# First of the four additions over the states by an accumulating DMA issued from the Pool engine; two state tiles, and the rest of each sum one chunk later

## The chip, the cores and the metric

One Trainium2 chip, one core. The metric is device microseconds of one execution of the whole program, the median of several runs. The core has five engines, each with a program of its own that runs in order: TensorE (PE), VectorE (DVE), ScalarE (ACT), GpSimd (POOL) and SyncE (SP, which here only issues DMAs). They meet through semaphores: `wait_ge(s, v)` holds an engine, and all that stands behind it there, until `s` has reached `v`.

## The reference, cut to what matters

Three blocks with residuals: attention to a context, a selective scan (Mamba), and a feed-forward block with quantised weights. The change is in the scan and at the three layer norms.

```python
x = x + attention(ctx, ctx, _layernorm(x), mask, ...)       # 64 sequences of 32, 257 keys, 16 heads of 32
x = x + mamba(_layernorm(x), ...)
x = x + ffn(_layernorm(x), ...)                             # 512 -> 2048 -> 512, quantised

# mamba: d_inner 1024, 16 states n for each channel d
dt  = softplus(bcd[..., -1:] * dt_w + dt_b)
dA  = exp(dt[..., None] * A)
dBx = (dt * x_)[..., None] * Bm[:, :, None, :]
def step(h, inp):
    dA_t, dBx_t, C_t = inp
    h = dA_t * h + dBx_t
    y_t = einsum('bdn,bn->bd', h, C_t)                      # the sum over the 16 states
    return (h, y_t)
y = (y + x_ * D) * silu(z);  out = y @ out_proj_w
```

## The kernel before, in words

**Tiles.** The 2048 rows are cut into 16 tiles of 128 rows, that is 4 sequences each. One tile passes attention, then the scan, then its output product. `schedule` is one list of steps that every engine walks in the same order, each doing its own part of a step (`part.x` does nothing on an engine that has no method of that name). `interval(ta, tm, to, more)` works at three tiles at once: attention of tile `ta`, the first part of the scan of `tm = ta - 1`, the end of the scan and the output of `to = ta - 2`. It has four quarters b = 0 to 3, one for each sequence. The intervals for `ta` = 0, 1, 2 are written out, 3 to 14 are a hardware loop, 15 is written out again, and two more intervals without attention empty the pipe. Afterwards the feed-forward block runs over all rows.

**The scan.** The 1024 channels of a tile are 8 chunks c of 128 channels, one for each partition. A chunk takes four steps on DVE, which this text calls:
- B(c), L1442: `hb` = u times the rows B, 128x2048 (16 states of 128 positions);
- S(c), L1446: the scan over `hb` in place with the decays `dA` of the chunk, 128x2048;
- C(c), L1451: `hb` times the rows C, 128x2048;
- sum(c), L1457 and L1461: the sum over the 16 states by four halvings, of 1024, 512, 256 and 128 elements; the last writes `u`.

There is one `hb`, so the 32 steps of a tile run strictly one after the other (step k is step k % 4 of chunk k // 4). The decays are 16 exponentials of 128x124 a chunk on ACT (`decays`, L1141), in two tiles `dA`: those of chunk c wait for S(c - 2).

**Where the steps stand.** `place(name)` is called at named points of a quarter, and two tables say which scan steps stand there: `BEGIN` holds steps 0 to 13 of tile `tm` (from quarter 2 on), `FINISH` holds steps 14 to 31 of tile `to` (from quarter 0 on). The other DVE work between them is the attention's scores (`score_pass`, L1353, four passes with the key mask `maskn`) and reciprocals, `x1_write` (L1380, the attention's output plus the residual), the layer norm statistics (L1273, L1278), the convolution (L1407, 24 small instructions), `mamba_steps` (L1415, the 8 products that open the time steps dt) and `mamba_dt` (L1421, L1426), which closes them and makes `u`, and `mamba_gated` (L1468, L1471).

**Layer norm.** DVE takes the statistics of 128 rows, POOL makes scale and offset from them (`rstd`: L1187, L1189, L1192, three instructions on 128x1), ACT normalises the rows into one third of `ln_out` (L1019), and PE transposes them. The norm ahead of the scan (index 1) stands in quarter 0: `x1_write`, statistics, `rstd`, ACT, transpose (L867), the product with `win_sb` (`in_product`, L874), ACT's copies and first taps (L1088), DVE's convolution. POOL also scales the key mask once a quarter (L1201), adds the residual's bias (L1215), and copies x1 into x2 (`mamba_keep`, L1241), for which the next `x1_write` waits.

**The row dt.** In quarter 1 `mamba_bcd` copies the small product (L1101) and SP sends it to DRAM and its last row back to all partitions (`BC`, 64 KB), which `mamba_steps` in quarter 2 reads.

```python
for b in range(BT):
    ...
    if b == 0 and front: part.mamba_norm(tm)
    place("a")
    if here: part.softmax(g)
    place("m")
    if b == 0 and front: part.mamba_rows(tm)
```

## Time and profile before

| | us |
|---|---|
| median of 3 runs (lowest, highest) | 2366.3 (2363.32, 2367.36) |
| the profiled execution, its own time | 2362.47 |
| its span, first to last instruction | 2360.7 |
| DVE busy | 2020.6 (86% of the span) |
| PE busy | 1942.2 (82%) |
| ACT busy | 1676.1 (71%) |
| POOL busy | 344.0 (15%) |
| granted TensorE clock, mean | 0.914 of full speed |
| DMA queue q1, share of 16 engines' time | 17.8% |

All durations come from the one profiled execution; what lies around its span is 1.8 us. In forty equal slices of it DVE is busy 90% or more from the fifth slice to the thirty-seventh nearly throughout, and PE, with 80 to 99%, is hardly less so until the attention ends. With three engines so full, the share of busy time doesn't tell which one sets the pace: the chain of waits and the engines' timelines over one interval do. The timelines below are those of one pass of the loop, between 1170 and 1300 us, and of the last two intervals, after 2018 us. All passes of the loop look alike.

### The profile page before, as it was taken

How to read it: one execution, taken by the hardware profiler on the slowest of the kernel's cores; microseconds unless marked ns; L12 is line 12 of the kernel's file. 1: busy time of each engine (PE TensorE's matmuls, PEld its weight loads, DVE VectorE, ACT ScalarE, POOL GpSimd, SP SyncE). 2: the span in 40 equal slices, each digit the busy share in tenths (PEclk: the TensorE clock that was granted, in tenths of full speed). 3: DMA queues.
4: the chain of work that ended last, by engine and by line, in shares of the span. 5: the costliest groups of instructions: out<-in, count | busy, mean ns of one | idle time of the engine just before them, and what ended most of it. 6: DMA issues, size and time to landing. Idle time of an engine off the chain costs nothing.

```text
span 2360.7 us, 36464 instructions
## 1 busy us (share of the span) xinstructions
PE 1942.2 (82%) x11244; PEld 1371.5 (58%) x11244; DVE 2020.6 (86%) x2429; ACT 1676.1 (71%) x4598; POOL 344.0 (15%) x296
## 2 busy tenths in 40 slices
PE   6998898989798888989898989798888987430678
PEld 5676566666575666666666666575656665320233
DVE  1534989999999999999999999999999999899577
ACT  2457787877878787778787877878887878653391
POOL 1000121121211111111111111212111111000003
PEclk9999998989999999989999989999999998765789
DMA  7521010111111101112121211111111211210113
GB/s 224 221 74 65 25 66 26 64 37 60 41 55 39 46 37 36 64 37 64 34 66 25 64 37 60 41 60 34 48 36 35 64 32 42 77 42 22 56 37 120
DMA packets 81206, 136.48 MB, mean 58 GB/s; under 512 B 17408, under 2 KB 40592, under 8 KB 75920
## 3 DMA queue, kind: packets, MB, share of 16 engines
q1 hardware_dynamic: 81040, 134.89, 17.8%
q14 instruction: 138, 1.13, 0.2%
q8 instruction: 28, 0.46, 0.1%
HBM read 117.69 MB, written 17.18 MB: 57 GB/s over the span
## 4 chain that ended last, share of the span: by engine, by line
DVE 31%; ACT 23%; PE 15%; issue 12%; DMA 3%; POOL 2%; DVEq 1%; ACTq 0%; SPq 0%; POOLq 0%
ACT dA L1141 10%; DVE hb L1446 10%; PE bank L874 6%; DVE hb L1457 5%; DVE hb L1451 5%; DVE hb L1442 3%; PE bank L944 2%; PE bank L784 2%; DVE xs L1407 2%; DMA BC<-bcd_dram 2%; ACT Pr L1012 2%; ACT Pr L1045 2%; PE bank L954 1%; ACT KT L990 1%; DVE dt L1415 1%
## 5 line engine op out<-in xcount | busy, mean ns | idle before, releaser
L1141 ACT ACTIVATE dA<-dt,A_sb 128x124 f32<-128x124 f32 x2048 | 610.6, 390 | 91.7 <-DVE dt L1421 58.6
L1446 DVE TENSOR_TENSOR_SCAN hb<-dA,hb 128x2048 f32<-128x2048 f32 x128 | 566.1, 4423 | 21.4 <-ACT dA L1141 17.1
L775 PE MATMUL bank<-ctxT,wk_sb 128*128 128x256 f32 x2048 | 489.1, 398 | 65.3 <-ACT ctxT L982 62.8
L775 PEld LDWEIGHTS bank<-ctxT,wk_sb 128*128 128x128 f32 x2048 | 403.2, 200 | 139.2 <-ACT ctxT L982 60.4
L784 PE MATMUL bank<-wv_sb,ctxT 128*128 128x512 f32 x1024 | 462.1, 594 | 0.9 <-ACT ctxT L982 0.9
L1457 DVE TENSOR_TENSOR hb<-hb 128x1024 f32<-128x1024 f32 (+2 forms) x384 | 301.8, 786 | 12.2
L1451 DVE TENSOR_TENSOR hb<-hb,BC 128x2048 f32<-128x2048 f32 x128 | 296.9, 2319 | 6.3 <-issue 3.4
L874 PE MATMUL bank<-xn2T,win_sb 128*128 128x128 f32 x2048 | 269.5, 299 | 36.0 <-ACT xn2T L1070 31.7
L784 PEld LDWEIGHTS bank<-wv_sb,ctxT 128*128 128x128 f32 x1024 | 186.4, 191 | 193.8 <-issue 192.5
L1442 DVE TENSOR_TENSOR hb<-u,BC 128x2048 f32<-128x2048 f32 x128 | 293.2, 2291 | 3.4
L874 PEld LDWEIGHTS bank<-xn2T,win_sb 128*128 128x128 f32 x2048 | 266.2, 215 | 41.6 <-ACT xn2T L1070 36.2
L1187 POOL TENSOR_SCALAR stats<-stats 128x1 f32<-128x1 f32 x48 | 68.1, 1419 | 1028.4 <-DVE stats L1278 1028.4
L908 PE MATMUL bank<-wout_sb,zs 128*128 128x512 f32 x256 | 118.4, 617 | 95.0 <-DVE zs L1471 95.0
L1012 ACT ACTIVATE Pr<-Pr,soft 128x257 f32<-128x257 f32 x256 | 127.3, 508 | 48.6 <-DVE soft L1353 48.6
L990 ACT ACTIVATE KT<-bank,bqkv 128x256 f32<-128x256 f32 x256 | 106.4, 466 | 56.5 <-PE bank L775 54.9
L997 ACT COPY V<-bank 128x512 f32<-128x512 f32 x128 | 74.8, 584 | 101.0 <-PE bank L821 76.7
L1353 DVE CUSTOM_DVE_ANT_0 Pr<-bank,maskn 128x257 f32<-128x257 f32 x256 | 94.2, 421 | 61.0 <-PE bank L803 39.3
L821 PEld LDWEIGHTS bank<-PT,V 128*128 128x128 f32 x1024 | 125.9, 194 | 31.3 <-issue 31.3
L1201 POOL TENSOR_SCALAR maskn<-maskb 128x257 f32<-128x257 f32 x64 | 87.4, 1366 | 378.0 <-DVE soft L1353 365.2
L1407 DVE SCALAR_TENSOR_TENSOR xs<-xpad,convw,xs 128x128 f32<-128x128 f32 x384 | 106.3, 346 | 40.8 <-ACT xs L1088 39.5
L908 PEld LDWEIGHTS bank<-wout_sb,zs 128*128 128x128 f32 x256 | 49.5, 199 | 152.8 <-DVE zs L1471 95.6
L821 PE MATMUL bank<-PT,V 128*128 128x128 f32 x1024 | 126.4, 277 | 0.8 <-ACT PT L1062 0.8
(131 smaller groups left out, 2357.6 us busy)
## 6 DMA issues: line engine op xcount, KB each, us to landing
ctx_sb<-in_ctx_dram SPq DMA_DIRECT2D x64, 512.0 KB, 3.7
BC<-bcd_dram SPq DMA_DIRECT2D x32, 1024.0 KB, 4.9
maskb<-in_mask_Bx1x1xS_fk_dram SPq DMA_DIRECT2D x64, 128.5 KB, 3.3
wstage<-in_L_ffn_w_dram SPq DMA_DIRECT2D x4, 2048.0 KB, 10.6
x_sb<-in_x_dram SPq DMA_DIRECT2D x16, 256.0 KB, 3.4
win_sb<-in_L_attn_in_proj_w_dram SPq DMA_DIRECT2D x1, 4096.0 KB, 25.2
bo_sb<-bias_dram SPq DMA_DIRECT2D x64, 64.0 KB, 2.1
x_dram<-x SPq DMA_DIRECT2D x16, 256.0 KB, 2.1
```

The source lines that it names most:

```text
L775: last = pe.matmul(bank[6 + j][:, (m % 2) * KF:(m % 2 + 1) * KF], wk_sb[:, c, m * P:(m + 1) * P], ctxT[:, c, :], start=(c == 0), stop=(c = ...
L784: last = pe.matmul(bank[h][:], ctxT[:, c, h * P:(h + 1) * P], wv_sb[:, c, :], start=(c == 0), stop=(c == DC - 1))
L821: last = pe.matmul(bank[4][:, m * P:(m + 1) * P], V[:, h, m * P:(m + 1) * P], PT[:, h, m, :], start=(h == 0), stop=(h == 1))
L874: last = pe.matmul(bank[6 + q % 2][:, e * P:(e + 1) * P], win_sb[:, c, n:n + P], xn2T[:, c, :], start=(c == 0), stop=(c == DC - 1))
L908: last = pe.matmul(bank[5][:], zs[:, c, :], wout_sb[:, c, :], start=(c == 0), stop=(c == IC - 1))
L1012: act.activation(Pr[:, m, :], Pr[:, m, :], ACT.Exp, scale=-1.0, bias=soft[:, 0, m:m + 1], accum_out=soft[:, 1, m:m + 1]).then_inc(exp_done, 1)
L1141: last = act.activation(dA[:, c % 2, n * BT:(n + 1) * BT, 1:], dt[:, c, :].rearrange("p (b s) -> p b s", s=S)[:, :, 1:], ACT.Exp, scale=A_ ...
L1407: dve.scalar_tensor_tensor(acc, src, tap, acc, ALU.mult, ALU.add).then_inc(conv_done, 1)
L1442: ins = dve.tensor_tensor(hb[:], u[:, c, :].unsqueeze(1).broadcast_to([P, NS, P]), BC[:, 0:NS, :], ALU.mult)
L1446: ins = dve.tensor_tensor_scan(flat, dA[:, c % 2].rearrange("p n s -> p (n s)"), flat, 0.0, ALU.mult, ALU.add)
L1451: ins = dve.tensor_tensor(hb[:], hb[:], BC[:, NS:2 * NS, :], ALU.mult)
L1457: dve.tensor_tensor(hb[:, 0:n, :], hb[:, 0:n, :], hb[:, n:2 * n, :], ALU.add).then_inc(sum_step, 1)
```

## The change

- A second state tile: `hb` is `[P, 2, NS, P]`, and chunk c works in tile c % 2.
- After C(c), for c = 0 to 6, POOL issues a DMA that adds the upper eight states of the tile to the lower eight (source and target 128x1024 in fp32, that is 512 KB read, and 512 KB read and written again). DVE's sum(c) starts with the halving of 512 and waits for that DMA's semaphore `hb_added`. For chunk 7 (`whole`) all four additions stay on DVE.
- A new order of the 32 steps, `CHAIN`: B(c), S(c), sum(c - 1), C(c). The tables `BEGIN` and `FINISH` are rewritten for it, and the waits that counted steps go by `DONE`.
- To make room, `ln_out` has one third of its size and the three layer norms take turns in it, with waits for the transposes that read it; the unused space `apart` goes; `last_vT` and `bias_rows` move into x1 and x2.
- The load of the first block of the feed-forward input moves from ahead of the last interval into it.

```diff
--- before.py
+++ after.py
-        ln_out = sb("ln_out", [P, 3, D])
+        ln_out = sb("ln_out", [P, D])
...
-        sb("apart", [P, 800])
 
         dA = sb("dA", [P, 2, NS * BT, S])
-        hb = sb("hb", [P, NS, P])
+        hb = sb("hb", [P, 2, NS, P])
-        last_vT = ln_out[:, 2, 0:DC * B].rearrange("p (m b) -> p m b", b=B)
-        bias_rows = ln_out[0:B, 1, :]
-        hb_words = hb[:].rearrange("p n q -> p (n q)").bitcast(BF16)
+        last_vT = x1[:, 0:DC * B].rearrange("p (m b) -> p m b", b=B)
+        bias_rows = x2[0:B, :]
+        hb_words = hb[:, 0].rearrange("p n q -> p (n q)").bitcast(BF16)
...
+        CHAIN = [(0, 0), (0, 1), (0, 2)]
+        for c in range(1, IC):
+            CHAIN += [(c, 0), (c, 1), (c - 1, 3), (c, 2)]
+        CHAIN.append((IC - 1, 3))
+        DONE = {step: k + 1 for k, step in enumerate(CHAIN)}
...
-        FINISH = {(0, "a"): range(14, 15), (0, "b"): range(15, 17), (0, "c"): range(17, 21), (0, "e"): range(21, 22),
+        FINISH = {(0, "a"): range(14, 15), (0, "b"): range(15, 16), (0, "c"): range(16, 20), (0, "e"): range(20, 22),
...
+                    if b == 2 and back and not front:
+                        part.ffn_prefetch()
...
-                        sp.wait_ge(scan_step, 4 * IC * t - 3 + 2 * i)
+                        sp.wait_ge(scan_step, 4 * IC * (t - 1) + DONE[IC - 1, 2 * i])
...
+                    sp.wait_ge(scan_step, 4 * IC * (NT - 1) + DONE[IC - 1, 1])
                     sp.dma_start(xblk[:], xn3_dram[:, :, 0:TB]).then_inc(xb_loaded, 16)
...
-                def layernorm_rows(self, i, t, rows, used):
+                def layernorm_rows(self, i, t, rows):
                     act.wait_ge(ln_rstd[i], 3 * (t + 1))
-
-                    wait(act, used, t)
-                    act.activation(ln_out[:, i, :], rows, ACT.Identity, scale=stats[:, i, 9:10],
+                    act.activation(ln_out[:], rows, ACT.Identity, scale=stats[:, i, 9:10],
                                    bias=stats[:, i, 10:11]).then_inc(ln_done[i], 1)
 
                 def ln_q_rows(self, t):
-                    self.layernorm_rows(0, t, x_sb[:], xnT_psum)
+                    wait(act, xn2T_psum, t - 1)
+                    self.layernorm_rows(0, t, x_sb[:])
 
                 def mamba_rows(self, t):
                     if isinstance(t, int) and t == 0:
                         act.wait_ge(bias_stored, 16)
-                    self.layernorm_rows(1, t, x1[:], xn2T_psum)
+                    wait(act, xnT_psum, tiles(t + 2))
+                    wait(act, xn3T_psum, t - 1)
+                    self.layernorm_rows(1, t, x1[:])
 
                 def out_rows(self, t):
-                    self.layernorm_rows(2, t, x2[:], xn3T_psum)
+                    wait(act, xnT_psum, tiles(t + 4))
+                    wait(act, xn2T_psum, tiles(t + 2))
+                    wait(act, xn3T_psum, t)
+                    self.layernorm_rows(2, t, x2[:])
...
-                                act.wait_ge(scan_step, 4 * IC * t + 4 * (c - 2) + 2)
+                                act.wait_ge(scan_step, 4 * IC * t + DONE[c - 2, 1])
                             elif not first:
-                                act.wait_ge(scan_step, 4 * IC * t - 6 + 4 * c)
+                                act.wait_ge(scan_step, 4 * IC * (t - 1) + DONE[IC - 2 + c, 1])
...
+                def scans(self, t, steps):
+                    for k in steps:
+                        c, op = CHAIN[k]
+                        if op == 2 and not whole(c):
+                            pool.wait_ge(scan_step, 4 * IC * t + k + 1)
+                            apart(pool)
+                            pool.dma_start(hb[:, c % 2, 0:NS // 2, :], hb[:, c % 2, NS // 2:NS, :], accum_op=ALU.add
+                                           ).then_inc(hb_added, 16)
+
...
-                    flat = hb[:].rearrange("p n q -> p (n q)")
                     for k in steps:
-                        c = k // 4
-                        if k == 0:
-                            dve.wait_ge(u_ready, 2 * (t + 1))
-                            dve.wait_ge(bc_loaded[0], 16 * (t + 1))
-                            if isinstance(t, int) and t == 0:
-                                dve.wait_ge(wq_stored[3], 16)
-                        else:
-                            dve.wait_ge(scan_step, 4 * IC * t + k)
-                        if k % 4 == 0:
-                            ins = dve.tensor_tensor(hb[:], u[:, c, :].unsqueeze(1).broadcast_to([P, NS, P]),
+                        c, op = CHAIN[k]
+                        tile = hb[:, c % 2]
+                        flat = tile.rearrange("p n q -> p (n q)")
+                        if op == 0:
+                            if c == 0:
+                                dve.wait_ge(u_ready, 2 * (t + 1))
+                                dve.wait_ge(bc_loaded[0], 16 * (t + 1))
+                                if isinstance(t, int) and t == 0:
+                                    dve.wait_ge(wq_stored[3], 16)
+                            if c >= 2:
+                                dve.wait_ge(scan_step, 4 * IC * t + DONE[c - 2, 3])
+                            elif not (isinstance(t, int) and t == 0):
+                                dve.wait_ge(scan_step, 4 * IC * (t - 1) + DONE[IC - 2 + c, 3])
+                            ins = dve.tensor_tensor(tile, u[:, c, :].unsqueeze(1).broadcast_to([P, NS, P]),
                                                     BC[:, 0:NS, :], ALU.mult)
-                        elif k % 4 == 1:
+                        elif op == 1:
+                            dve.wait_ge(scan_step, 4 * IC * t + DONE[c, 0])
                             dve.wait_ge(dA_ready, IC * t + c + 1)
                             ins = dve.tensor_tensor_scan(flat, dA[:, c % 2].rearrange("p n s -> p (n s)"), flat, 0.0,
                                                          ALU.mult, ALU.add)
-                        elif k % 4 == 2:
-                            if k == 2:
+                        elif op == 2:
+                            dve.wait_ge(scan_step, 4 * IC * t + DONE[c, 1])
+                            if c == 0:
                                 dve.wait_ge(bc_loaded[1], 16 * (t + 1))
-                            ins = dve.tensor_tensor(hb[:], hb[:], BC[:, NS:2 * NS, :], ALU.mult)
+                            ins = dve.tensor_tensor(tile, tile, BC[:, NS:2 * NS, :], ALU.mult)
                         else:
-                            n = NS // 2
-                            for level in range(3):
-                                if level:
-                                    dve.wait_ge(sum_step, 3 * (IC * t + c) + level)
-                                dve.tensor_tensor(hb[:, 0:n, :], hb[:, 0:n, :], hb[:, n:2 * n, :], ALU.add
+                            dve.wait_ge(scan_step, 4 * IC * t + DONE[c, 2])
+                            if not whole(c):
+                                dve.wait_ge(hb_added, 16 * ((IC - 1) * t + c + 1))
+                            n = NS // 2 if whole(c) else NS // 4
+                            done = (2 * IC + 1) * t + 2 * c
+                            while n > 1:
+                                dve.tensor_tensor(tile[:, 0:n, :], tile[:, 0:n, :], tile[:, n:2 * n, :], ALU.add
                                                   ).then_inc(sum_step, 1)
+                                done += 1
+                                dve.wait_ge(sum_step, done)
                                 n //= 2
-                            dve.wait_ge(sum_step, 3 * (IC * t + c + 1))
-                            ins = dve.tensor_tensor(u[:, c, :], hb[:, 0, :], hb[:, 1, :], ALU.add)
+                            ins = dve.tensor_tensor(u[:, c, :], tile[:, 0, :], tile[:, 1, :], ALU.add)
                         ins.then_inc(scan_step, 1)
```

Three places in the order. First DVE in quarter 0, from the statistics of x1 on (tile `to` = 2 tiles back: C(3) comes first). Before:

```order
L1278 BN_AGGR stats<-stats 128x2
L1451 TENSOR_TENSOR hb<-hb,BC 128x2048
L1366 RECIPROCAL soft<-soft 128x4
L1457 TENSOR_TENSOR hb<-hb 128x1024
L1457 TENSOR_TENSOR hb<-hb 128x512
L1457 TENSOR_TENSOR hb<-hb 128x256
L1461 TENSOR_TENSOR u<-hb 128x128
L1442 TENSOR_TENSOR hb<-u,BC 128x2048
L1446 SCALAR_TENSOR_TENSOR hb<-dA,hb 128x2048
```

And in the changed kernel, where L1483 is C, L1472 is B, L1477 is S, and L1491 and L1496 are the sum:

```order
L1306 BN_AGGR stats<-stats 128x2
L1483 TENSOR_TENSOR hb<-hb,BC 128x2048
L1394 RECIPROCAL soft<-soft 128x4
L1472 TENSOR_TENSOR hb<-u,BC 128x2048
L1477 SCALAR_TENSOR_TENSOR hb<-dA,hb 128x2048
L1491 TENSOR_TENSOR hb<-hb 128x512
L1491 TENSOR_TENSOR hb<-hb 128x256
L1496 TENSOR_TENSOR u<-hb 128x128
L1483 TENSOR_TENSOR hb<-hb,BC 128x2048
L1472 TENSOR_TENSOR hb<-u,BC 128x2048
L1435 SCALAR_TENSOR_TENSOR xs<-xpad,convw,xs 128x128 x24
L1477 SCALAR_TENSOR_TENSOR hb<-dA,hb 128x2048
```

The four short additions of sum(3) behind C(3) have given way to B(4) and S(4), and sum(4), which stood ahead of the convolution, now stands behind it, ahead of the next scores. Second DVE in quarter 2, from the opening of dt to `mamba_gated`. Before:

```order
L1415 TENSOR_SCALAR dt<-BC,chan 128x128 x8
L1446 SCALAR_TENSOR_TENSOR hb<-dA,hb 128x2048
L1451 TENSOR_TENSOR hb<-hb,BC 128x2048
L1457 TENSOR_TENSOR hb<-hb 128x1024
L1457 TENSOR_TENSOR hb<-hb 128x512
L1457 TENSOR_TENSOR hb<-hb 128x256
L1461 TENSOR_TENSOR u<-hb 128x128
L1468 TENSOR_TENSOR u<-u,xD 128x1024
```

Now (L1443 is the opening of dt, L1503 the first of `mamba_gated`):

```order
L1443 TENSOR_SCALAR dt<-BC,chan 128x128 x8
L1477 SCALAR_TENSOR_TENSOR hb<-dA,hb 128x2048
L1491 TENSOR_TENSOR hb<-hb 128x512
L1491 TENSOR_TENSOR hb<-hb 128x256
L1496 TENSOR_TENSOR u<-hb 128x128
L1483 TENSOR_TENSOR hb<-hb,BC 128x2048
L1491 TENSOR_TENSOR hb<-hb 128x1024
L1491 TENSOR_TENSOR hb<-hb 128x512
L1491 TENSOR_TENSOR hb<-hb 128x256
L1496 TENSOR_TENSOR u<-hb 128x128
L1503 TENSOR_TENSOR u<-u,xD 128x1024
```

The sum of chunk 6 has come in behind S(7), and chunk 7 keeps all four of its additions. Third POOL in quarter 0 of the changed kernel (L1204 to L1209 are `rstd`, L1218 the mask, L1250 the zeros of the padding):

```order
L1232 TENSOR_TENSOR xbo<-x_sb,bo_sb 128x512
L1204 TENSOR_SCALAR stats<-stats 128x1
L1206 TENSOR_TENSOR stats<-stats,consts 128x1
L1209 TENSOR_SCALAR stats<-stats 128x1
L1243 DMA hb<-hb 128x1024
L1218 TENSOR_SCALAR maskn<-maskb 128x257
L1250 MEMSET xpad 128x32x3
L1243 DMA hb<-hb 128x1024
```

Before, the same stretch has the same rows without the two DMAs: the one for chunk 3 stands behind `rstd`, and the mask behind it.

## Rows read from the trace of the kernel before

**Rows 1.** The page: the chain that ended last, by engine and by line.

```profile
DVE 31%; ACT 23%; PE 15%; issue 12%; DMA 3%; POOL 2%; DVEq 1%; ACTq 0%; SPq 0%; POOLq 0%
ACT dA L1141 10%; DVE hb L1446 10%; PE bank L874 6%; DVE hb L1457 5%; DVE hb L1451 5%; DVE hb L1442 3%; PE bank L944 2%; PE bank L784 2%; DVE xs L1407 2%; DMA BC<-bcd_dram 2%; ACT Pr L1012 2%; ACT Pr L1045 2%; PE bank L954 1%; ACT KT L990 1%; DVE dt L1415 1%
```

**Rows 2.** Groups by line and form, DVE: busy us, mean ns, idle before.

```profile
L1457 DVE TENSOR_TENSOR hb<-hb 128x1024 f32<-128x1024 f32 x128 | 157.8, 1233 | 3.4
L1457 DVE TENSOR_TENSOR hb<-hb 128x512 f32<-128x512 f32 x128 | 88.6, 692 | 4.4
L1457 DVE TENSOR_TENSOR hb<-hb 128x256 f32<-128x256 f32 x128 | 55.4, 432 | 4.4
L1461 DVE TENSOR_TENSOR u<-hb 128x128 f32<-128x128 f32 x128 | 38.6, 301 | 4.4
```

**Rows 3.** Timeline of DVE, quarter 0: start us, duration us.

```profile
1266.20 0.66 DVE L1380 TENSOR_TENSOR x<-bank,xbo 128x512 f32<-128x512 f32 x1
...
1270.55 2.29 DVE L1451 TENSOR_TENSOR hb<-hb,BC 128x2048 f32<-128x2048 f32 x1
...
1272.87 2.41 DVE L1457 TENSOR_TENSOR hb<-hb 128x1024 f32<-128x1024 f32 x3
...
1275.72 2.29 DVE L1442 TENSOR_TENSOR hb<-u,BC 128x2048 f32<-128x2048 f32 x1
1278.13 4.42 DVE L1446 TENSOR_TENSOR_SCAN hb<-dA,hb 128x2048 f32<-128x2048 f32 x1
...
1291.08 6.74 DVE L1407 SCALAR_TENSOR_TENSOR xs<-xpad,convw,xs 128x128 f32<-128x128 f32 x24 [1.09 <-ACT xs L1088]
```

**Rows 4.** Timeline of POOL, quarters 3 and 0, and after the last scan.

```profile
1240.83 1.87 POOL L1241 COPY x<-x 128x512 f32<-128x512 f32 x1 [4.39 <-ACT ln_out L1019]
...
1270.87 2.05 POOL L1187 TENSOR_SCALAR stats<-stats 128x1 f32<-128x1 f32 x1 [0.81 <-DVE stats L1278]
1273.00 1.52 POOL L1189 TENSOR_TENSOR stats<-stats,consts 128x1 f32<-128x1 f32 x1
1274.73 0.27 POOL L1192 TENSOR_SCALAR stats<-stats 128x1 f32<-128x1 f32 x1 [0.21 <-POOL stats L1189]
...
2206.86 0.27 POOL L1192 TENSOR_SCALAR stats<-stats 128x1 f32<-128x1 f32 x1 [0.21 <-POOL stats L1189]
```

**Rows 5.** One line of POOL, `mamba_keep`: shortest, median and longest in ns.

```profile
L1241 POOL COPY x<-x x16: 611/1868/1871, 225.1 to 2109.5; 128x512 f32<-128x512 f32 x16
```

**Rows 6.** Timeline of ACT: the normalised rows of the scan's layer norm.

```profile
1275.12 0.81 ACT L1019 ACTIVATE ln_out<-x,stats 128x512 f32<-128x512 f32 x1 [4.38 <-POOL stats L1192]
```

**Rows 7.** Timeline of DVE, quarters 1 and 2.

```profile
1171.25 4.42 DVE L1446 TENSOR_TENSOR_SCAN hb<-dA,hb 128x2048 f32<-128x2048 f32 x1
1175.58 0.40 DVE L1353 CUSTOM_DVE_ANT_0 Pr<-bank,maskn 128x257 f32<-128x257 f32 x1
...
1201.21 2.14 DVE L1415 TENSOR_SCALAR dt<-BC,chan 128x128 f32<-128x128 f32 x8 [1.67 <-DMA BC<-bcd_dram]
```

**Rows 8.** Timeline of PE, quarter 1: the transposes of the attention weights.

```profile
1181.76 1.80 PE L812 MATMUL bank<-idf,Pr 128*128 128x128 f32 x8
```

**Rows 9.** Timeline of ACT, quarters 2 and 3: decays of chunks 0 and 2.

```profile
1216.03 4.74 ACT L1141 ACTIVATE dA<-dt,A_sb 128x124 f32<-128x124 f32 x16 [3.84 <-DVE dt L1421]
...
1247.29 2.43 ACT L1141 ACTIVATE dA<-dt,A_sb 128x124 f32<-128x124 f32 x8
```

**Rows 10.** Timeline of DVE, quarter 3: scans of chunks 1 and 2.

```profile
1237.87 4.42 DVE L1446 TENSOR_TENSOR_SCAN hb<-dA,hb 128x2048 f32<-128x2048 f32 x1
...
1249.98 4.42 DVE L1446 TENSOR_TENSOR_SCAN hb<-dA,hb 128x2048 f32<-128x2048 f32 x1
```

**Rows 11.** Timeline of DVE, the intervals without attention: scan of the last tile's chunk 1.

```profile
2110.11 4.41 DVE L1446 TENSOR_TENSOR_SCAN hb<-dA,hb 128x2048 f32<-128x2048 f32 x1
```

**Rows 12.** The page, DMA issues: KB each, us from issue to landing.

```profile
ctx_sb<-in_ctx_dram SPq DMA_DIRECT2D x64, 512.0 KB, 3.7
BC<-bcd_dram SPq DMA_DIRECT2D x32, 1024.0 KB, 4.9
```

30 lines of the change are left out of this document (18 added, 12 removed).

## The prediction, made before the changed kernel had run

> **What bounds the kernel now.** I read the chain of waits first, since three engines are full. It is spread over all of them: DVE holds 31% of the chain, ACT 23%, PE 15%, and the costliest line of each has 6 to 10%. The sums, L1457, have 5% [rows 1]. So no engine is the bound throughout: an interval is a relay, and an instruction taken off DVE is worth something only where DVE holds the baton. Then I went through the timelines of one pass of the loop, to see who holds it when. The reader should find four stretches.
>
> - Quarter 0, from `x1_write` to the convolution. DVE writes x1 and takes the statistics; POOL makes scale and offset, 1270.87 to 1275.00; ACT has sat idle 4.38 us for them [rows 4, 6]; PE's transposes, its product and ACT's taps follow, and DVE waits 1.09 us before the convolution [rows 3]. The relay goes DVE, POOL, ACT, PE, ACT; the scan steps of DVE only fill time.
> - Convolution to opening of dt. DVE runs S(5), then the scores at 1175.58; exponentials, transposes (at 1181.76) and ACT's copies follow, then the row dt goes through DRAM, and DVE waits 1.67 us for it [rows 7, 8]. DVE holds the baton only up to the scores.
> - Opening of dt to its closing: DVE alone, and ACT waits 3.84 us for the result [rows 9]. Then ACT works without a gap (its timeline shows none) until the exponentials that let S(1) start at 1237.87.
> - S(1) to `x1_write`: DVE without a gap, 1237.87 to 1266.20 [rows 3, 10].
>
> **The change, part by part.** The first addition takes 1.233 us, and 7 x 16 = 112 go: 138 us of DVE's time. A shortened sum costs 0.69 + 0.43 + 0.30 us with some 0.03 between: 1.5 us; a whole one 2.8 [rows 2]. Now stretch by stretch.
>
> *POOL behind DVE's long steps (quarter 0).* A POOL instruction that reads the state buffer doesn't end while DVE runs an instruction with two operands there. L1187 starts at 1270.87 and ends at 1272.92, C(3) runs from 1270.55 to 1272.84; L1189 ends at 1274.52, 0.4 us behind the first addition (1272.87 + 1.23 = 1274.10); L1192 needs 0.27 us when nothing runs [rows 3, 4]. A scan does the same: `mamba_keep` starts at 1240.83 within the scan that ends at 1237.87 + 4.42 = 1242.29, and ends at 1242.70; its median is 1.87 us, its shortest 0.61 [rows 4, 5, 10]. In the new order B(4) and S(4) stand behind C(3) instead of short additions. So L1189 meets B(4), 1272.87 to 1275.16, and ends at about 1275.6. L1192 comes 0.2 us later, meets S(4), which then runs to 1279.7, and ends at about 1279.8, against 1275.00. The whole relay waits for it: 4.8 us in each of the 14 intervals `ta` = 2 to 15 (the earlier ones have no sum in quarter 0), and in the one after them: 15 x 4.8 = 72 us. Bounds: 0, if the instruction slips in between B(4) and S(4), and 4.9. I take 4.8, after the copy, whose median of 16 is the blocked time.
>
> The Trainium skill, "SBUF — State Buffer", section "Who interferes with whom", says that a DVE instruction with two inputs in SBUF contends with a GpSimd instruction that reads SBUF, and that the second to issue blocks until the first has finished. The scan has two. By this rule L1192 would wait it out and the 72 us would stand; if only multiplications and additions blocked, the sum would be the 38 us of the second rival. The trace agrees with the rule for the copy (ended 0.41 us behind the scan).
>
> What was DVE's own in this stretch falls away into waiting: 1.2 us of sum(3) and 2.8 of sum(4), beside the 1.09 it waits already. The DMA for chunk 3 stands behind L1192 on POOL, so it is issued at about 1279.9 and sum(3) starts near 1286; with 1.5 + 2.3 + 2.3 us behind it DVE is ready by 1292, ahead of the convolution at 1291.1 + 4.8 = 1295.9. Covered for a DMA up to 10 us.
>
> *sum(4) ahead of the scores.* It used to hide ahead of the convolution; now its 1.5 us stand between S(5) and the scores, on the relay: 14 x 1.5 = 21 us. The savings of sum(5) and sum(6) further on lie beside the transposes and the row dt: nothing.
>
> *sum(6) behind S(7).* 1.5 us more between opening and closing of dt, where ACT waits: 15 x 1.5 = 23 us.
>
> *S(1) to `x1_write`.* Three short sums (4.5 us) stand where two whole ones (5.6) did: DVE could be 1 us earlier. But S(2) needs its decays, and ACT ends them at 1247.29 + 2.43 = 1249.72; S(2) started at 1249.98 [rows 9, 10]. From 1249.8 on: 4.4 + 1.5 + 2.3 + 2.3 + 4.4 + 1.5 = 16.4, so `x1_write` at 1266.3 or so: +0.1 to +0.2, 3 us in all. `mamba_keep` now stands behind the DMA of chunk 2 and may meet S(3); it then ends near 1265.3, 1 us ahead of need.
>
> *The end.* In the first interval without attention two sums between convolution and dt are shortened and one comes in; between 0 and -2.5, as the row dt is nearly as late: -1.5. sum(0) leaves the stretch ahead of S(1) (0 to -2.8, since POOL's norm is waited for): -1.5. From S(1) of the last tile, 2110.11 [rows 11], only DVE works: six sums lose 1.23 us each, sum(0) comes in with 1.5: -5.9. Together -9.
>
> *The DMA itself* isn't in the trace. It reads 512 KB twice and writes 512: between a plain load of 512 KB, 3.7 us, and twice that, 7.4; nearest is the row that moves 1024 KB in 4.9 [rows 12]; I take 6 with its issue from POOL. Behind C(c) stand B and S of the next chunk, 6.7 us: covered. Each microsecond above 6.7 costs one in quarter 3 of 15 intervals and in each of seven sums at the end, 22 us. By "DMA: Bandwidth & Descriptors" of the Trainium skill (section on the SWDGE path), 2.0 us + bytes / 436 GB/s, it would be an estimated 3.2 us for 512 KB; no run here shows it. The DMA for chunk 6 can also share the queues with the row dt: 0 to 1.5 us x 14, I take 0.
>
> The shared `ln_out`: each new wait is for a transpose at least one quarter back: nothing. The moved load of the feed-forward input is issued some 20 us ahead of its use: nothing.
>
> Sum: 72 + 21 + 23 + 3 - 9 = 110 us on the profiled execution's own 2362.5, so 2472.5; the median of before is 4 us above that execution, within the spread of its three runs. I forecast 2473.
>
> **The rivals.**
> - *Faster: DVE's time comes back where it is on the chain.* L1457 has 5% of it, 118 us, of which the first addition has 157.8 / 301.8; seven of eight go: 54 us, 2309. It decides if the moved sums find cover that I don't see. Against it: ACT waits for DVE in the very stretch that gets longer [rows 9].
> - *POOL slips in.* L1192 is served between B(4) and S(4): 110 - 72 = 38 us, 2401. For it: the instruction needs only 0.27 us. Against: it comes 0.2 us after L1189 ends, and S(4) starts before.
> - *The accumulating DMA is slow.* At 9 us it adds 2.3 x 22 = 50: 2523. Nothing in the trace speaks to it but the bound of 7.4, which gives 2488.
> - *No change*: the losses of sum(4) and sum(6) are absorbed and POOL slips in: 2360 to 2370.
>
> **How the numbers follow.** Forecast 0.56, POOL slips in 0.14, slow DMA 0.14, faster 0.12, no change 0.04. The forecast's own range is 2440 to 2495. The whole reaches down to the POOL rival, with some of the other sums absorbed, and up to the bound of the DMA with the row dt disturbed (2488 + 21): 2388 to 2510. Faster by over 0.2% (about what a measurement of this kernel can tell): 0.12; within: 0.04; slower: 0.84.
>
> **What would show it.** In quarter 0 the last `rstd` instruction lasts about 4 us and ends just behind a scan, and ACT's wait ahead of `ln_out` grows from 4.4 to 9 us; DVE waits over 5 us ahead of the convolution; ACT waits 5.3 us for the closing of dt; S(2) waits 1 us for its decays; an interval grows by 8 us; the 112 DMAs land within 7 us and DVE's wait for them is short except at sum(3). Wrong if DVE has little idle time and the interval is shorter, or if DVE's waits go to the DMA.

## The result: 7.9% slower, in the predicted direction and by more than predicted

| kernel | median us | runs from to | ratio to before, 95% |
|---|---|---|---|
| before | 2364.8 | 2362.8 to 2367.4 | |
| changed | 2551.4 | 2543.6 to 2557.8 | 1.0787 [1.0753, 1.0821] |

The forecast was 2473, its range ended at 2510. The loss is 187 us where the sum had 110. The four runs of the changed kernel spread over 14 us, so a difference against it stands within some 8 us. The profiled execution of the changed kernel took 2554.0 us, its span 2552.1.

The page of the changed kernel:

```profile
PE 1990.1 (78%) x11244; PEld 1399.3 (55%) x11244; DVE 1853.1 (73%) x2317; ACT 1678.0 (66%) x4598; POOL 556.0 (22%) x408
...
ACT 24%; PE 20%; DVE 20%; issue 16%; POOL 5%; DMA 4%; DVEq 1%; ACTq 0%; SPq 0%; POOLq 0%
...
L1491 DVE TENSOR_TENSOR hb<-hb 128x512 f32<-128x512 f32 (+2 forms) x272 | 160.3, 589 | 147.5 <-DMA hb<-hb 142.1
...
L1030 ACT ACTIVATE ln_out<-x,stats 128x512 f32<-128x512 f32 x32 | 26.0, 812 | 184.2 <-POOL stats L1209 184.2
...
hb<-hb POOLq DMA_DIRECT2D x112, 512.0 KB, 4.8
```

The first additions on DVE fell from 157.8 to 19.6 us, the 138 us that were to go, and DVE's share of the chain fell from 31 to 20% [rows 1]. What grew is "issue" (12 to 16%), PE (15 to 20%) and POOL (2 to 5%). The accumulating DMA is quick, 4.8 us in the median and 7.0 at most.

Where in the loop the time went is read from the starts of six DVE instructions in each of twelve intervals, `ta` = 4 to 15 (mean us; the differences of starts are worked out from the timelines). Eleven of the twelve are passes that the loop's jump led into, the last is written out. S(0) is the first scan of the new tile.

| kernel | x1_write to conv. | conv. to scores 1 | to opening of dt | to closing | to S(0) | to x1_write | interval |
|---|---|---|---|---|---|---|---|
| before | 24.78 | 10.99 | 25.26 | 14.01 | 5.64 | 45.17 | 125.84 |
| changed | 30.74 | 12.66 | 28.49 | 15.25 | 5.62 | 47.64 | 140.41 |
| change | +5.96 | +1.67 | +3.23 | +1.24 | 0 | +2.47 | +14.57 |

The prediction had +4.8, +1.5, 0, +1.5, 0 and +0.2. So four columns hold, the first of them with 1.2 us too much, and two are wrong: the way to the opening of dt and the way to `x1_write`.

Quarter 0 in the changed kernel, DVE, to be held against [rows 3]:

```profile
1382.38 0.29 DVE L1496 TENSOR_TENSOR u<-hb 128x128 f32<-128x128 f32 x1
1385.74 0.69 DVE L1408 TENSOR_TENSOR x<-bank,xbo 128x512 f32<-128x512 f32 x1 [3.07 <-issue]
...
1391.29 2.29 DVE L1483 TENSOR_TENSOR hb<-hb,BC 128x2048 f32<-128x2048 f32 x1
...
1395.97 4.42 DVE L1477 TENSOR_TENSOR_SCAN hb<-dA,hb 128x2048 f32<-128x2048 f32 x1
1405.56 1.15 DVE L1491 TENSOR_TENSOR hb<-hb 128x512 f32<-128x512 f32 x2 [5.16 <-DMA hb<-hb]
...
1416.90 6.74 DVE L1435 SCALAR_TENSOR_TENSOR xs<-xpad,convw,xs 128x128 f32<-128x128 f32 x24 [5.46 <-ACT xs L1105]
```

The same moment on POOL and on ACT [rows 4, 6]:

```profile
1391.62 2.04 POOL L1204 TENSOR_SCALAR stats<-stats 128x1 f32<-128x1 f32 x1 [3.59 <-DVE stats L1306]
1393.75 2.53 POOL L1206 TENSOR_TENSOR stats<-stats,consts 128x1 f32<-128x1 f32 x1
1396.48 3.98 POOL L1209 TENSOR_SCALAR stats<-stats 128x1 f32<-128x1 f32 x1 [0.21 <-POOL stats L1206]
1400.41 0.94 POOL L1243 DMA_DIRECT2D hb<-hb  x1
```

```profile
1400.50 0.81 ACT L1030 ACTIVATE ln_out<-x,stats 128x512 f32<-128x512 f32 x1 [9.02 <-POOL stats L1209]
```

This is the predicted picture: the last `rstd` instruction lasts 3.98 us and ends 0.07 us behind S(4) (1395.97 + 4.42 = 1400.39), ACT waits 9.0 us instead of 4.4, DVE waits 5.5 ahead of the convolution. In the mean of the twelve intervals POOL's norm ends 9.15 us behind the statistics, 4.45 before the change: 4.7 us, where the prediction had 4.8. The other 1.2 us of the column stand ahead of the statistics. There lies what was not predicted: 3.07 us of idle "issue" between the end of sum(2), the last DVE instruction of the loop's body, and `x1_write`, and a second gap of 2.50 us behind `x1_write`, ahead of the scores. Before the change there was no gap ahead of `x1_write`, and the one behind it was 1.2 us shorter:

```profile
1141.50 0.43 DVE L1353 CUSTOM_DVE_ANT_0 Pr<-bank,maskn 128x257 f32<-128x257 f32 x1 [1.27 <-issue]
```

One of the prediction's signs failed outright: DVE's waits for the DMAs were to be short except at sum(3), but sum(5) waits nearly as long (4.87 us in the pass shown further on).

### The profile page after: what moved, and what is told of

Read it like the earlier page. It is cut to its first block, busy times and chain, and to the rows that moved or that the text cites. A ratio compares the mean times of both kernels' runs of the same rounds, so it can differ in the third digit from the quotient of the medians.

```text
span 2552.1 us, 36715 instructions
## 1 busy us (share of the span) xinstructions
PE 1990.1 (78%) x11244; PEld 1399.3 (55%) x11244; DVE 1853.1 (73%) x2317; ACT 1678.0 (66%) x4598; POOL 556.0 (22%) x408
## 4 chain that ended last, share of the span: by engine, by line
ACT 24%; PE 20%; DVE 20%; issue 16%; POOL 5%; DMA 4%; DVEq 1%; ACTq 0%; SPq 0%; POOLq 0%
ACT dA L1158 11%; DVE hb L1477 6%; PE bank L887 6%; DVE hb L1491 4%; PE bank L797 3%; PE bank L788 3%; POOL stats L1209 2%; PE bank L957 2%; DVE xs L1435 2%; DMA BC<-bcd_dram 2%; PE bank L967 2%; DMA bcd_dram<-bcd 2%; DVE hb L1472 2%; ACT KT L1003 2%; PE bank L868 2%
## 5 line engine op out<-in xcount | busy, mean ns | idle before, releaser
L1477 DVE TENSOR_TENSOR_SCAN hb<-dA,hb 128x2048 f32<-128x2048 f32 x128 | 570.9, 4460 | 45.4 <-ACT dA L1158 37.7
L797 PE MATMUL bank<-wv_sb,ctxT 128*128 128x512 f32 x1024 | 479.3, 613 | 0.9 <-ACT ctxT L995 0.9
L797 PEld LDWEIGHTS bank<-wv_sb,ctxT 128*128 128x128 f32 x1024 | 193.3, 198 | 204.8 <-issue 203.5
L1483 DVE TENSOR_TENSOR hb<-hb,BC 128x2048 f32<-128x2048 f32 x128 | 293.8, 2295 | 0.0
L1472 DVE TENSOR_TENSOR hb<-u,BC 128x2048 f32<-128x2048 f32 x128 | 291.9, 2281 | 1.7
L1204 POOL TENSOR_SCALAR stats<-stats 128x1 f32<-128x1 f32 x48 | 91.4, 1904 | 875.9 <-DVE stats L1306 875.8
L1491 DVE TENSOR_TENSOR hb<-hb 128x512 f32<-128x512 f32 (+2 forms) x272 | 160.3, 589 | 147.5 <-DMA hb<-hb 142.1
L1243 POOL DMA_DIRECT2D hb<-hb x112 | 100.9, 901 | 711.9 <-DVE hb L1483 703.2
L880 PE MATMUL bank<-idf,ln_out 128*128 128x128 f32 x64 | 17.3, 424 | 168.4 <-ACT KT L1003 138.5
L1030 ACT ACTIVATE ln_out<-x,stats 128x512 f32<-128x512 f32 x32 | 26.0, 812 | 184.2 <-POOL stats L1209 184.2
```

The costliest lines, as they stand in the source:

```text
L797: last = pe.matmul(bank[h][:], ctxT[:, c, h * P:(h + 1) * P], wv_sb[:, c, :], start=(c == 0), stop=(c == DC - 1))
L1472: ins = dve.tensor_tensor(tile, u[:, c, :].unsqueeze(1).broadcast_to([P, NS, P]), BC[:, 0:NS, :], ALU.mult)
L1477: ins = dve.tensor_tensor_scan(flat, dA[:, c % 2].rearrange("p n s -> p (n s)"), flat, 0.0, ALU.mult, ALU.add)
L1483: ins = dve.tensor_tensor(tile, tile, BC[:, NS:2 * NS, :], ALU.mult)
L1491: dve.tensor_tensor(tile[:, 0:n, :], tile[:, 0:n, :], tile[:, n:2 * n, :], ALU.add).then_inc(sum_step, 1)
```

## The experiments

Every kernel ran beside the kernel before on its chip, whose medians were 2362.9 to 2366.5 us.

**One wait more at the norm.** DVE's B(4) waits for POOL's `rstd`, so that only C(3) can block POOL.

```diff
+                            if c == 4 and not (isinstance(t, int) and t == NT - 1):
+                                dve.wait_ge(ln_rstd[1], 3 * (t + 2))
```

> The changed kernel with one wait more: DVE starts B(4) only when POOL has ended the scan's layer norm. No work is taken away, and the chunk's steps start later. Theory (POOL's small instructions are held up by B(4) and S(4)): the last of them lasts 0.27 us again instead of 3.98, the norm is ready 5.7 us earlier, ACT's wait ahead of ln_out falls from 9.0 to about 3.5 us, and 15 x 5.7 = 85 us go: 2466 (2450 to 2485). Rival (the accumulating DMA is what costs, by DVE's wait at sum(3) or by its traffic): DVE starts later still, so the time stays at 2551 or rises.

2443.9 us, 1.0352 [1.0334, 1.0370]: 107.5 us back by holding DVE still, more than the range expected (2450 at least). POOL in that kernel:

```profile
1326.87 2.04 POOL L1204 TENSOR_SCALAR stats<-stats 128x1 f32<-128x1 f32 x1 [3.89 <-DVE stats L1306]
1329.00 0.57 POOL L1206 TENSOR_TENSOR stats<-stats,consts 128x1 f32<-128x1 f32 x1
1329.78 0.27 POOL L1209 TENSOR_SCALAR stats<-stats 128x1 f32<-128x1 f32 x1 [0.21 <-POOL stats L1206]
```

The last two steps fell from 2.53 and 3.98 us to 0.57 and 0.27, so DVE's instructions stretch POOL's. 5.7 of the 7.7 us per interval came back in quarter 0 (25.04 instead of 30.74). That is 1 us more than the order had cost there, because the norm now ends 3.5 us behind the statistics, and 4.45 in the kernel before. 2.3 more came back on the way to dt (26.22 instead of 28.49), which I had not expected; where from is told with sum(4) below.

**sum(2) moved** from the end of quarter 3 to behind x1's statistics, so that the loop's body ends with S(3) again.

```diff
-        FINISH = {(0, "a"): range(14, 15), ...
+        FINISH = {(0, "a"): range(13, 15), ...
-                 ... (3, "e"): range(10, 14)}
+                 ... (3, "e"): range(10, 13)}
```

> The changed kernel with sum(2) taken from the end of quarter 3 to quarter 0, behind the statistics of x1, so that DVE's part of the loop ends with S(3) again. Theory: the gap of the loop's jump lies under the scan again (3.1 us ahead of x1_write and 1.2 ahead of the scores, 12 times: 51 us), sum(2) is off the way to x1_write (15 x about 1 us), and POOL meets short additions first and then C(3) only (15 x 5.1 = 77 us): about -143, 2408 (2390 to 2430). Rival (the jump costs the same wherever it stands; the gap ahead of x1_write is a wait for data): the pool term and the 15 us alone, 2460.

2394.6 us, 1.0126 [1.0103, 1.0149], in the range expected: 157 us of the 187 are back by the place of one short sum. x1_write to convolution is 24.97 us, S(0) to `x1_write` 44.22. The gap ahead of `x1_write` is 0.1 us. The way to dt is 26.73, 1.8 less than in the changed kernel, which belongs to the same unexpected part as the 2.3 above.

**The DMA of chunk 6 held back** until the row dt has landed.

```diff
+                            if c == 6 and not (isinstance(t, int) and t == NT - 1):
+                                pool.wait_ge(dtrow_loaded, 16 * (t + 2))
```

> The changed kernel with one wait more on POOL: the accumulating DMA of chunk 6 is issued only when the row dt of the next tile has landed. Theory (this DMA shares the queues with the 16.5 KB store and the 64 KB load of the row dt, on the relay): the way from the copy of bcd to the opening of dt falls from 7.6 to 5.6 us, 14 x 2.0 = 28 us, 2523. The DMA then has 6.5 us until sum(6), and lands in 5.7. Rival (the row dt is late because of other loads, the context's above all): no change, 2551, or a few us more by a wait at sum(6).

2532.2 us, 1.0714 [1.0696, 1.0732], 19 us below the changed kernel, and 9 above what was expected. From ACT's bcd copy (its copy of the small product, of which the row dt is a part) to the opening of dt the profiled pass took 5.57 us, against 7.60 (1308.94 to 1316.54) in the changed kernel: the accumulating DMA disturbs the small transfers beside it, for 1.7 us of the 3.2 in that column.

**The new order without the DMA**: all four additions on DVE.

```diff
         def whole(c):
-            return c == IC - 1
+            return True
```

> The changed kernel without any accumulating DMA: all four additions of every chunk on DVE, in the new order, with two state tiles. Theory (the order costs, the DMA pays a little back): DVE gets 1.24 us more in sum(4) (14 times) and sum(6) (15 times), about 2.3 us more between S(1) and x1_write (14 times) and 9 us at the end, and the row dt is 2 us earlier (14 times): +50, 2600 (2570 to 2620). Rival (the DMA itself is the loss): well below 2551, towards 2400.

2607.3 us, 1.1039 [1.1021, 1.1057]. The DMA is worth 56 us to the changed kernel, so the loss is not the DMA's. That it is the order's, and not that of the shared `ln_out`, is shown by the kernel with all three sums moved, below.

**The kernel before, with one wait at the loop's end**: DVE waits for its own S(3) before it takes the jump.

```diff
                         ins.then_inc(scan_step, 1)
+                        if k == 13 and not isinstance(t, int):
+                            dve.wait_ge(scan_step, 4 * IC * t + 14)
```

> The kernel before, and one wait of DVE added behind the last scan step of the loop (B(3) and S(3) are done before DVE's sequencer takes the loop's jump), so that the jump's gap no longer lies under the 4.4 us of S(3). Nothing is computed otherwise. Theory (the jump shows where the loop does not end with a long DVE instruction; it was 3.07 us of idle ahead of x1_write and up to 2.5 us more before the softmax in the changed kernel): 3 to 4.3 us in each of 12 passes, so 2400 to 2415 us. Rival (the jump costs no time, x1_write waits for PE there in any case, and the time of the changed kernel went elsewhere): 2363, within 5.

2411.0 us, 1.0191 [1.0174, 1.0208]: 46 us, nothing computed otherwise. The line of `x1_write`, durations in ns and what ended the idle time before it, between 500 and 2000 us of this kernel's span:

```profile
L1380 DVE TENSOR_TENSOR x<-bank,xbo x12: 691/692/693, 516.2 to 1950.6; 128x512 f32<-128x512 f32 x12
its engine sat idle before it (us, times) until:
  issue: 38.1, 11
```

In the kernel before there is no idle time ahead of that line. 38.1 / 11 = 3.5 us per pass; the interval grew by 3.94, 3.18 of them up to `x1_write` and 0.70 behind it. The wait alone is not the cause: of the twelve `x1_write`, eleven come behind a jump back, and the twelfth, behind the loop's last pass, has no such gap, in this kernel and in the changed one. So the jump costs 3 to 3.5 us in both, where DVE has nothing long running while its sequencer makes it. What the sequencer does in that time no run here shows.

**sum(4) moved** from ahead of the scores of quarter 1 to behind them, in the changed kernel.

```diff
-        FINISH = {... (0, "e"): range(20, 22),
-                  (1, "a"): range(22, 23), ...
+        FINISH = {... (0, "e"): range(20, 21),
+                  (1, "a"): range(21, 23), ...
```

> The changed kernel with sum(4) alone moved, from ahead of the scores of quarter 1 to behind them. With both sums moved the interval was 5.2 us shorter than in the changed kernel: 1.7 of it between the convolution and the scores, 1.2 between the opening and the closing of dt (sum(6)), 2.5 between the scores and the opening of dt. Theory (a pause of TensorE costs its clock too: in the changed kernel it waits 1.37 us for the softmax of quarter 1, where the kernel before does not wait, and then the 8 transposes and 8 products take 1.97 to 2.53 and 4.61 to 5.29 us instead of 1.80 and 3.60; without sum(4) ahead of the scores neither is seen): 1.7 + 1.3 to 1.5 us in each of 14 intervals, 42 to 45 less, 2507 (2502 to 2514), conv to scores 11.0 us, TensorE's pair 1.8 and 3.6. Rival (sum(4) costs its own 1.7 us only, the slow products lie beside other waits): 23 less, 2528 (2523 to 2533).

2490.3 us, 1.0521 [1.0504, 1.0538]: 61 us, more than either theory had (45 at most). The columns: 1.68 less between convolution and scores, as expected, and 2.46 less up to the opening of dt. The reason is in POOL's line of quarter 1, the norm of x. First the changed kernel:

```profile
1289.95 2.06 POOL L1204 TENSOR_SCALAR stats<-stats 128x1 f32<-128x1 f32 x1 [20.57 <-DVE stats L1306]
1292.09 2.53 POOL L1206 TENSOR_TENSOR stats<-stats,consts 128x1 f32<-128x1 f32 x1
1294.83 3.97 POOL L1209 TENSOR_SCALAR stats<-stats 128x1 f32<-128x1 f32 x1 [0.21 <-POOL stats L1206]
1298.75 0.93 POOL L1243 DMA_DIRECT2D hb<-hb  x1
...
1307.87 0.88 POOL L1243 DMA_DIRECT2D hb<-hb  x1 [7.70 <-DVE hb L1483]
```

Then the one with sum(4) behind the scores:

```profile
1256.52 2.02 POOL L1209 TENSOR_SCALAR stats<-stats 128x1 f32<-128x1 f32 x1 [0.21 <-POOL stats L1206]
1258.99 0.94 POOL L1243 DMA_DIRECT2D hb<-hb  x1 [0.45 <-issue]
...
1269.38 0.88 POOL L1243 DMA_DIRECT2D hb<-hb  x1 [8.43 <-DVE hb L1483]
```

Quarter 0's accident happens a second time: statistics, then C, B and S without a short sum between. Nobody waits for that norm here, but POOL's next instruction is the issue of chunk 5's DMA. It comes at 1298.75, 6.8 us behind the end of C(5), so DVE stands 4.87 us at sum(5), C(6) is late, and the DMA of chunk 6 is issued 1.1 us ahead of the bcd copy (1308.94) instead of 3.8 us ahead of it (1269.38 to 1273.16). DVE in the changed kernel:

```profile
1289.63 2.29 DVE L1483 TENSOR_TENSOR hb<-hb,BC 128x2048 f32<-128x2048 f32 x1
...
1303.61 1.15 DVE L1491 TENSOR_TENSOR hb<-hb 128x512 f32<-128x512 f32 x2 [4.87 <-DMA hb<-hb]
...
1316.54 1.63 DVE L1443 TENSOR_SCALAR dt<-BC,chan 128x128 f32<-128x128 f32 x6 [3.73 <-DMA BC<-bcd_dram]
```

With sum(4) moved the wait for the row is 1.75 us and the way from the copy to dt 5.63 us (1273.16 to 1278.79). In the mean of the twelve intervals that way is 7.0 us in the changed kernel and 5.3 with sum(4) moved, 1.7 of the 2.46. The other 0.7 us stand ahead of the copy, where PE is slower: in the changed kernel

```profile
1293.34 2.53 PE L825 MATMUL bank<-idf,Pr 128*128 128x128 f32 x8 [1.38 <-ACT Pr L1062]
1295.66 4.61 PE L797 MATMUL bank<-wv_sb,ctxT 128*128 128x512 f32 x8
```

against 1.97 and 3.60 with sum(4) moved. That part of the theory stands, at half of the size I gave it. It does not happen in every pass: behind the same 1.38 us of idle the products took 3.60 us in one pass of the changed kernel and 4.6 to 5.3 in the ten others, and in the kernel with the wait at B(4) 3.60 in six passes and 4.9 to 5.3 in five.

The place of sum(4) is not the whole cause of that accident. The kernel with the wait at B(4) has sum(4) where the changed kernel has it, and the same order of DVE in quarter 1, and yet its POOL is early there. POOL, then DVE's C(5), in a pass of that kernel:

```profile
1228.26 0.23 POOL L1204 TENSOR_SCALAR stats<-stats 128x1 f32<-128x1 f32 x1 [20.01 <-DVE stats L1306]
...
1232.95 0.94 POOL L1243 DMA_DIRECT2D hb<-hb  x1
```

```profile
1228.31 2.29 DVE L1485 TENSOR_TENSOR hb<-hb,BC 128x2048 f32<-128x2048 f32 x1 [0.28 <-issue]
```

C(5) comes 0.3 us later there, just behind the start of POOL's first step, which lasts 0.23 us and not 2.06; the DMA of chunk 5 is issued 4.1 us earlier and sum(5) waits 0.15 us for it. The kernel with sum(2) moved shows the same. In both the way from the copy to dt is 5.3 us, though neither touches the DMA of chunk 6. This is the unexpected part of what those two gave back. Why C(5) stands 0.28 us in them and not in the changed kernel stays open. So of the 61 us a part is the price of a coincidence of 0.3 us. Where the coincidence was gone already, in the kernel with sum(2) moved, moving sum(4) and sum(6) together gave 40 us (below), and the prediction's terms for the two come to 44.

**sum(4) and sum(6) moved**; sum(6) goes ahead of S(7), in front of the opening of dt, where DVE waits in any case.

```diff
+        CHAIN[28:30] = [(IC - 2, 3), (IC - 1, 1)]
-                  (2, "a"): range(27, 28), (2, "b"): range(28, 31), ...
+                  (2, "a"): range(27, 29), (2, "b"): range(29, 31), ...
```

> The changed kernel with two of its sums elsewhere and sum(2) left at the loop's end: sum(4) behind the scores, sum(6) ahead of S(7) in front of the opening of dt. The two steps of the prediction were 1.5 us in 14 and 15 intervals: 2551 - 21 - 23 = 2507 (2500 to 2515). With sum(2) mended first the same two moves gave 40.2 us. Rival (behind POOL's late rstd they do not lie on the path): 2540 to 2551.

2487.3 us, 1.0519 [1.0504, 1.0533], below the range expected (2500 at least), since it had 21 us for sum(4). Against the kernel with sum(4) moved alone (1.0521) this is nothing that can be told from the noise. Opening to closing of dt did shrink, 15.25 to 14.01, but S(0) to `x1_write` grew from 47.69 to 48.31: half is given back within the same pass. What is left, 0.6 us in an interval, goes at the end: there the last S(7) stands behind sum(6) and its DMA, starts 14.6 us behind S(6) instead of 10.3, and the time behind the last `x1_write` grows from 332.6 to 340.5 us.

**All three sums moved.**

> The changed kernel with three of its sums elsewhere: sum(2) behind x1's statistics as in the run with sum(2) alone (2394.6), sum(4) behind the scores instead of ahead of them, sum(6) ahead of S(7), in front of the opening of dt, where DVE waits 3.7 us for the row in any case. By the steps of the prediction, whose terms were 1.5 us in each of 14 and 15 intervals for these two sums: 2395 - 21 - 22 = 2352, 2345 to 2365. Rival (at both places DVE has slack now, the order of the short sums costs nothing by itself): 2390 to 2400.

2354.5 us, 0.9959 [0.9943, 0.9974], as expected: the order was the whole loss, since the DMA, the second tile and the shared `ln_out` are all still there, and the change's idea now gains 10 us.

**And one wait at C(3).**

```diff
                         elif op == 2:
                             dve.wait_ge(scan_step, 4 * IC * t + DONE[c, 1])
+                            if c == 3 and not (isinstance(t, int) and t == NT - 1):
+                                dve.wait_ge(ln_rstd[1], 3 * (t + 2))
```

> The kernel with the three sums moved, and one wait: DVE's C(3), the first long step behind x1's statistics, waits until POOL has written the rstd of the norm ahead of the scan. With sum(2) moved alone POOL's last step still took 1.69 us and ended at 1306.63, behind C(3), where it would end near 1305.3 by its length with DVE still. If the norm's path sets the interval, 1 to 1.4 us less in each of 15 intervals: 15 to 20 us below the kernel without the wait, about 2335 (2325 to 2345). Rival (DVE is what bounds that stretch; C(3) is about 1 us later): 0 to 15 us above it.

2323.0 us, 0.9823 [0.9805, 0.9840], the fastest kernel of this study, 42 us below before; 31 from the wait, more than the 15 to 20 expected. In the twelve intervals the wait gives 1.3 us each, as expected, 15.5 in all. 7.3 more come from a single place, the loop's first pass. POOL there without the wait, its second step alone 4.76 us:

```profile
389.60 2.25 POOL L1205 TENSOR_SCALAR stats<-stats 128x1 f32<-128x1 f32 x1
391.94 4.76 POOL L1207 TENSOR_TENSOR stats<-stats,consts 128x1 f32<-128x1 f32 x1
```

With the wait these are 0.23 and 0.57 us. The other 9 us lie ahead of the loop and behind the last `x1_write`. PE in the kernel with the wait, in a pass of quarter 0:

```profile
1259.49 0.60 PE L881 MATMUL bank<-idf,ln_out 128*128 128x128 f32 x4
1263.09 7.41 PE L888 MATMUL bank<-xn2T,win_sb 128*128 128x128 f32 x64 [2.99 <-ACT xn2T L1088]
```

The input product takes 7.41 us in this pass; in a pass of the kernel before it took 9.75 and in one of the changed kernel 10.00. The rows of these stretches give the granted clock:

```profile
1153.00:1162.00 9.00, 9.00 (x61) 9.00 (x62) 8.79 (x7) 4.98 (x17) 0.00 (x0) 0.74 0.00 0
```

```profile
1263.00:1270.00 7.00, 6.91 (x61) 6.91 (x62) 6.93 (x5) 5.14 (x18) 0.00 (x0) 1.00 0.48 103
```

(window, its length, busy time and instructions of PE, PEld, DVE, ACT, POOL, then the clock; before, then this kernel.) Before the change PE came into the product from 3.81 us of idle ahead of four transposes and 2.13 behind them, and ran part of it at the lower level, 1.2 GHz; here the transposes followed directly on a product, after which it waited 2.99 us, and the clock was full. This pass is one of the good ones: of twelve, five took 7.41 us at a clock of 1.00 and seven 9.04 at 0.81. Without the wait it was two of twelve at 1.00. The mean is 8.36 us with the wait, 8.82 without, 9.57 in the kernel before. So the clock is part of the gain, but the gain at the convolution is no larger than the norm's own lead: by the wait ACT's rows came 1.6 us earlier and the convolution 1.07. What the clock gave by itself was not tried apart.

**The same, with chunk 6 added by DVE alone.**

```diff
         def whole(c):
-            return c == IC - 1
+            return c >= IC - 2
```

> As the one with the wait at C(3), and chunk 6 is now added by DVE alone too, as chunk 7 is: no accumulating DMA beside the reload of BC and the row dt, whose way from the bcd copy to the opening of dt was 7.6 us beside the DMA of chunk 6 and 5.55 us without. DVE's sum(6) is about 1.1 us longer, in front of a wait. Theory (row dt disturbed): 1 to 2 us less in each of 14 intervals, 14 to 28 us below the one with the DMA of chunk 6. Rival (the longer sum takes what the row gives back): within 10 of it.

2335.7 us, 0.9868 [0.9846, 0.9891]: 13 us slower, not 14 to 28 faster. The row dt is no longer waited for (idle ahead of its opening 0.0 us in the twelve intervals together, 6.7 with the DMA), but the longer sum(6) itself now ends last there (scores to opening 26.65, with the DMA 26.06). Once the order is mended there is at most 0.6 us a pass left to save on the row.

**The same wait at C(3) in the kernel before.**

```diff
+                            if k == 14 and not (isinstance(t, int) and t == NT - 1):
+                                dve.wait_ge(ln_rstd[1], 3 * (t + 2))
```

> The kernel before, and the same wait as in the fastest version: DVE's C(3), the first long step behind x1's statistics, waits for POOL's rstd of the norm ahead of the scan. In the kernel before POOL's three steps take 2.05, 1.52 and 0.27 us from 1144.19 beside C(3); with DVE still they would take some 0.3, 0.6 and 0.3, as in the run with the wait at B(4). Theory (the norm's path sets that stretch in the old order too, so the wait's gain is not the new order's): 1.5 to 2.5 us in each of 15 intervals, 2325 to 2342. Rival (C(3) held 1.3 us is as dear as the gain, since DVE carries more there without the accumulating DMA): 2355 to 2370.

2386.6 us, 1.0088 [1.0074, 1.0102]: the wait that gains 31 us there costs 23 here, which neither theory had (2370 at most). DVE and PE in this kernel:

```profile
1293.56 2.29 DVE L1453 TENSOR_TENSOR hb<-hb,BC 128x2048 f32<-128x2048 f32 x1 [1.67 <-POOL stats L1192]
```

```profile
1199.99 2.53 PE L812 MATMUL bank<-idf,Pr 128*128 128x128 f32 x8 [2.46 <-ACT Pr L1045]
1202.31 5.66 PE L784 MATMUL bank<-wv_sb,ctxT 128*128 128x512 f32 x8
```

POOL is quick again, and the norm ready 2.6 us earlier, but DVE was needed: it loses 1.67 us at C(3), comes to the convolution without its 1.1 us of slack (x1_write to convolution +0.70), and the scores' softmax is late for PE. PE stands 2.46 us ahead of the transposes where it did not stand [rows 8], and in the four microseconds that follow its granted clock is 0.50, that is 1.2 GHz:

```profile
1200.00:1204.00 4.00, 4.00 (x10) 2.34 (x11) 3.86 (x5) 3.75 (x8) 1.36 (x3) 0.50 0.12 25
```

Transposes and products take 2.53 + 5.66 us instead of 1.80 + 3.60 (2.52 + 5.04 in the mean of the twelve intervals), and scores to opening of dt grew by 1.95.

**The fastest kernel without the DMA** (all four additions on DVE, same order and wait).

> The fastest version so far without the accumulating DMA: same order, same wait, all four additions on DVE. It tells what the DMA itself is worth in an order that costs nothing: between the changed kernel and the same without the DMA it was 56 us, 4.0 in each of 14 intervals. Theory (its worth does not depend on the order): 2323 + 56 = 2379 (2365 to 2395). Rival (the DMA is worth little once the order is mended; ACT and PE bound the interval): 2325 to 2340.

2408.5 us, 1.0188 [1.0174, 1.0202]: the DMA is worth 85 us there, 56 in the changed kernel's order. Both expectations were too low (2395 at most): what the DMA is worth does depend on the order. Without it the fastest order loses to the kernel before. One reading is that the DMA leaves DVE the time to stand still for POOL; that is argued, not tried apart.

## Why the prediction was right in direction and wrong in size

- *Relay.* Right. 138 us less work on DVE brought a loss while the order stood, and DVE's waits grew.
- *POOL behind DVE's long steps*: forecast 72 us. The mechanism is shown twice (by the wait, and by sum(2) between), and the size is right: 4.7 us from the statistics to the norm's end, x 15 = 70. The wait gave back 107.5, since it makes the norm 1 us quicker than it was before the change and since quarter 1 escaped its own blocking with it. The step stopped one norm too early: in quarter 1 the same blocking hits the issue of a DMA. I had counted what waits for POOL's result and not what is queued behind it on POOL.
- *S(1) to `x1_write`*: forecast 3 us. This is the first failed step. S(2) did wait, 1.40 us for its decays, and the DVE work added up as predicted. But the loop's body now ended with a sum of 1.5 us, and the sequencer's jump, hidden under the 4.42 us of S(3) before, showed: 3.1 us ahead of `x1_write` in each of 11 passes, and 1.2 more behind it. The prediction put this at nothing, without a word. A wait alone in the kernel before reproduced 46 us. The trace of before showed only the jump's tail, the 1.27 us of "issue" ahead of the scores.
- *sum(4) ahead of the scores*: forecast 21 us. 1.67 us in the column, as forecast. The second failed step is the sentence behind it, that what follows up to the row dt is "nothing": that column grew by 3.23 us, by the chain shown above: POOL's norm, the issue of chunk 5's DMA, C(6), the DMA of chunk 6 beside the row dt, and PE's clock. Moving sum(4) back gave 61 us. The chain hangs on C(5) starting 0.3 us ahead of POOL's first step, which nobody could have read from the trace of before: there POOL is first.
- *sum(6) behind S(7)*: forecast 23 us. The column moved by 1.24 us, as 15 x 1.24 = 19, but moving it beside sum(4) was worth nothing clear of noise: half of the gain was gone half an interval later, the rest at the end. An edit's price in one stretch is not its price in the pass.
- *The DMA itself*: forecast 6 us and covered. It takes 4.8. Disturbance of the row dt, forecast 0 to 1.5 us and taken as 0, is 1.8 us an interval (7.0 us of way instead of 5.2): above its own upper bound, and 19 us when taken away alone.
- *The end*: forecast -9 us. From the last `x1_write` to the end 341.8 us became 332.1: -9.7.

The losses overlap. Taken back one at a time they are 107.5 (POOL), 46 (jump, measured in the kernel before), 61 (sum(4)), 19 (chunk 6's DMA) and nothing clear (sum(6)); all three sums together gave back 197. The steps that the prediction priced came out at 4.7, 1.67 and 1.24 us where it had 4.8, 1.5 and 1.5; what it missed is what it had at nothing. "The DMA is slow" and "DVE's time comes back" are refuted by the 4.8 us and by the result; "POOL slips in" by the 3.98 us. The range missed because it had no case for a cost outside the steps that I had named.

## What to carry to other kernels

Look at what an engine does while its sequencer jumps back, and try its longest instruction at the end of a loop's body; on DVE a short one there showed 3 to 4 us in every pass. Where GpSimd makes small values beside a busy VectorE, put short VectorE instructions (or a wait) behind the statistics, and count everything that is queued on GpSimd behind them, DMA issues above all. Compare several passes before you trust one: the same order was 4.1 us early or late by 0.3 us in the start of one instruction. A wait that holds an engine still pays only where that engine has slack: the same line was worth -31 us in the new order with the accumulating DMA and +23 in the kernel before.
